# Turning tiles 2 to 15 of x on VectorE, from loads made in 32x32 blocks, instead of on TensorE

## What is computed

```
h  = cond(x);  x = x + ffn(h)          # layer 0: cond = x @ W.T + 2 * gated LoRA (top 2 of 8 experts);
                                       #          ffn  = LoRA of the top-1 expert of 8, rank 16
h  = cond(x);  x = x + ffn(h)          # layer 1: cond = x @ W.T + b + 2 * LoRA of the sequence's slot;
                                       #          ffn  = x @ W_base.T + b_base + 2 * gated LoRA (top 2 of 8)
```

## Time and profile before

| | |
|---|---|
| time before, median of 3 runs | 510.89 us (510.64 to 512.52) |
| span of the profiled execution | 509.9 us, 8653 instructions |
| TensorE matmul busy | 497.2 us (98%), 3119 instructions |
| VectorE busy | 269.8 us (53%), 839 instructions |
| ScalarE busy | 135.9 us (27%), 300 instructions |
| GpSimd busy | 9.5 us (2%), 18 instructions |
| mean traffic of the DMA queues | 79 GB/s; 30397 packets |

### The profile page before, as it was taken

The page is one execution under the profiler, slowest core; times in us unless marked ns, Lnnn a source line. Parts: engine busy times, 40 slices in busy tenths (PEclk is TensorE's granted clock), DMA queues, the critical chain, the costliest instruction groups (busy, mean ns, idle before and its releaser), DMA issues.

```text
span 509.9 us, 8653 instructions
## 1 busy us (share of the span) xinstructions
PE 497.2 (98%) x3119; PEld 475.4 (93%) x3119; DVE 269.8 (53%) x839; ACT 135.9 (27%) x300; POOL 9.5 (2%) x18
## 2 busy tenths in 40 slices
PE   5999999999999989999999999999999999999997
PEld 4977899999999889999999999999999999999997
DVE  3655865444448355465384475466548438446211
ACT  4454620111111332241141132223124113222111
POOL 2040000000000000000000000000000000000000
PEclk9998999999999999999999999999999999999999
DMA  7984722311111131113104104012210410201111
GB/s 236 343 266 154 210 91 84 125 41 42 41 41 47 43 102 46 42 43 105 42 5 144 42 3 145 0 43 65 79 41 2 146 42 3 62 1 45 57 42 41
DMA packets 30397, 40.22 MB, mean 79 GB/s; under 512 B 10487, under 2 KB 22529, under 8 KB 30238
## 3 DMA queue, kind: packets, MB, share of 16 engines
q1 hardware_dynamic: 30094, 39.25, 23.6%
q0 software_dynamic: 272, 0.56, 0.4%
HBM read 28.64 MB, written 11.16 MB: 78 GB/s over the span
## 4 chain that ended last, share of the span: by engine, by line
PE 95%; DMA 2%; DVE 1%; ACT 1%; issue 0%; SPq 0%; POOL 0%; DVEq 0%; ACTq 0%
PE banks L1002 28%; PE banks L1004 27%; PE banks L1003 27%; PE banks L1016 3%; PE banks L997 3%; PE banks L1167 2%; PE banks L1200 1%; DMA wraw<-in_L_cond_W_dram 1%; PE banks L1051 1%; DMA routers<-in_L_ffn_W_router_dram 1%; PE banks L1025 1%; PE banks L1151 0%; PE banks L1205 0%; DVE ws_lo L676 0%; PE banks L1210 0%
## 5 line engine op out<-in xcount | busy, mean ns | idle before, releaser
L1002 PE MATMUL banks<-Mhi,x1Thi 128*128 128x392 f32 x384 | 138.0, 359 | 2.0 <-DVE x1Tlo L676 1.5
L1003 PE MATMUL banks<-Mlo,x1Thi 128*128 128x392 f32 x384 | 130.6, 340 | 0.0
L1004 PE MATMUL banks<-Mhi,x1Tlo 128*128 128x392 f32 x384 | 130.5, 340 | 0.0
L1002 PEld LDWEIGHTS banks<-Mhi,x1Thi 128*128 128x128 f32 x384 | 72.3, 188 | 4.5 <-issue 2.5
L1002 PE MATMUL banks<-WbThi,ws_hi 128*128 128x392 f32 (+2 forms) x216 | 74.7, 346 | 0.0
L1004 PE MATMUL banks<-WbThi,ws_lo 128*128 128x392 f32 (+2 forms) x216 | 73.2, 339 | 0.0
L1003 PE MATMUL banks<-WbTlo,ws_hi 128*128 128x392 f32 (+2 forms) x216 | 73.0, 338 | 0.0
L1003 PEld LDWEIGHTS banks<-Mlo,x1Thi 128*128 128x128 f32 x384 | 72.5, 189 | 0.0
L1004 PEld LDWEIGHTS banks<-Mhi,x1Tlo 128*128 128x128 f32 x384 | 72.2, 188 | 0.0
L1004 PEld LDWEIGHTS banks<-WbThi,ws_lo 128*128 128x128 f32 x216 | 40.7, 188 | 3.2
L1003 PEld LDWEIGHTS banks<-WbTlo,ws_hi 128*128 128x128 f32 x216 | 40.7, 188 | 3.1
(11 more groups left out here) (186 smaller groups left out, 796.7 us busy)
## 6 DMA issues: line engine op xcount, KB each, us to landing
wraw<-in_L_cond_W_dram SPq DMA_DIRECT2D x16, 512.0 KB, 4.4
out_dram<-ybuf SPq DMA_DIRECT2D x15, 512.0 KB, 3.1
xin<-in_x_dram SPq DMA_DIRECT2D x13, 512.0 KB, 4.3
wraw<-in_L_ffn_W_base_dram SPq DMA_DIRECT2D x8, 512.0 KB, 6.5
xin_first<-in_x_dram SPq DMA_DIRECT2D x1, 1024.0 KB, 9.2
x1T_dram<-xin_first SPq DMA_DIRECT2D x1, 1024.0 KB, 3.9
wraw<-x1T_dram SPq DMA_DIRECT2D x2, 512.0 KB, 3.5
Fbuf<-fe_hi_dram SPq DMA_DIRECT2D x16, 64.0 KB
```

Of the source, the lines that this page charges most:

```text
L1002: pe.matmul(out_, l[0], r[0], start=start, stop=False, **kw)
L1003: pe.matmul(out_, l[0], r[1], start=False, stop=False, **kw)
L1004: return pe.matmul(out_, l[1], r[0], start=False, stop=stop, **kw)
```

## The change

- `load_x` and the load of `x2_early` become `load_blocks`: four DMAs for a tile, one for each column group j of 32 numbers. Partition j*32+r, and in it k, i, c, get row i*32+r, column k*128+j*32+c of the tile. Each piece read is 32 numbers (128 bytes), 4096 pieces for a tile.
- VectorE then turns a whole tile with one instruction (`turn_x`): a transpose in 32x32 blocks of 128x1024 numbers, written into one half of `x1_sums`. For tiles n and n+1 it stands behind `split(3)` with a wait for `x1T_lo` (all four quarters of the last pair are split); for tile 2 it stands ahead of the splits of x1 of tiles 0 and 1, behind `m_done` 24; for tile 3 where the low part was formed.
- ScalarE copies the high part from `x1_sums` (SBUF) and not from PSUM, two instructions for a tile as before. For tile n this now stands behind `wzT_part(m + 1)` and still ahead of `y_part(m + 1, 0)`.
- GpSimd forms the low part: 28 subtractions of 128x512. VectorE's 28 instructions for it are gone.
- `x1_add` is one instruction for a quarter, in place, since `x1_sums` already holds the tile of x (tiles 0 and 1 keep the old form as `x1_first`).
- TensorE's 112 transposes of tiles 2 to 15 are gone. In slot 0, `small0(a)` moves from behind step 3 to behind step 10, just ahead of the turning of `hg`.
- SP waits for `x_turned` instead of `tx_done` before a new load of x. `x2_early` gets memory of its own. The scratch area of software DMAs is set to 8192 bytes.

```diff
+            def load_blocks(tile, t, s):
+                src = block_rows(t)
+                for j in range(NJ):
+                    sp.dma_start(tile[j * BLK:(j + 1) * BLK, :].rearrange("r (k i c) -> r k i c", k=K, c=BLK), src[j])\
+                      .then_inc(s, 16)
...
             def load_x(t, turn):
-                sp.dma_start(xin[turn][:, :], xf[bass.ds(t * P, P), :]).then_inc(x_in[turn], 16)
+                load_blocks(xin[turn], t, x_in[turn])
...
+            with gp.Fori(1, NB) as i:
+                for half in range(2):
+                    for h in range(2):
+                        gp.wait_ge(xT_hi, i * 4 + half * 2 + h + 1)
+                        gp.tensor_tensor(half_tiles(xT_main[1], half, h), half_tiles(x1_sums, half, h),
+                                         half_tiles(xT_main[0], half, h).bitcast(F32), ALU.subtract).then_inc(xT_lo, 1)
...
+            def turn_x(t, half, src, s, n):
+
+                dve.wait_ge(s, n)
+                dve.transpose(half_of(x1_sums, half), src[:, :].rearrange("p (k c) -> p k c", k=K)).then_inc(x_turned, 1)
...
+            def x1_add(q, g, bank):
+
+                dve.wait_ge(x1w_done, q * 4 + g + 1)
+                dve.tensor_tensor(quarter(x1_sums, g), bank, quarter(x1_sums, g), ALU.add).then_inc(x1_sum, 1)
...
+            dve.wait_ge(m_done, 3 * K)
+            turn_x(2, 0, x2_early, x2_in, 64)
             for g in range(4):
-                if g == 2:
-                    xT_part(2, 0, xT_main, XT_EARLY)
                 x1T_part(0, 0, g, quarter(wraw[2 + g // 2], g % 2))
...
                     if first:
-                        xT_part(a + 1, 1, xT_main, XT_BANKS[1])
+                        turn_x(a + 1, 1, xin[1], x_in[1], 64)
...
                 if has_n:
-                    xT_part(n, 0, xT_main, XT_BANKS[0])
-                    xT_part(n + 1, 1, xT_main, XT_BANKS[1])
+                    dve.wait_ge(x1T_lo, q * 4 + 4)
+                    turn_x(n, 0, xin[0], x_in[0], b * 64 + 64)
+                    turn_x(n + 1, 1, xin[1], x_in[1], b * 64 + 128)
...
                 pe.wait_ge(as_lo, b + 1)
+                main_to(7)
                 if first:
-                    main_to(0)
                     small0(a, 0, xT_main)
-                main_to(7)
...
                 adapter(m + 1)
-                main_to(40)
-                if has_n:
-                    turn_x_main(n, 0, b + 1, [(x1_half, q * 4 + 2), (x1_half, q * 4 + 3)])
                 main_to(44 if has_n else 46)
...
                 lora(m + 1, 1)
-                if has_n:
-                    turn_x_main(n + 1, 1, b + 2, [(x1_half, q * 4 + 4), (xT_lo, n * 2 + 1)])
                 main_to(48)
```

More of the change, by code:

```diff
@@ L87, in adaln_ffn @@
         wzThi, wzTlo = sb("wzThi", [P, P], F32R), sb("wzTlo", [P, P], F32R)
+        x2_early = sb("x2_early", [P, D])
         def gate_tiles(n):
@@ L268, in adaln_ffn @@
         c0_sums = [t[:, 0:4 * RC].rearrange("p (k c) -> p k c", k=4) for t in (a0f, b1_j)]
[L270 removed]
         XT_FIRST = [(pm[0], pm[1]), (pm[2], pm[0])]
[L272 removed]
+        BLK = 32
+        NJ = P // BLK
         X1W_BANKS, X1W_FIRST = [big[0], big[1], big[2], big[0]], [big[0], big[1], p0, pt]
@@ L283, in half_tiles, with block_rows, half_of @@
             return t[:, :].rearrange("p (k c) -> p k c", k=K)[:, 4 * h:4 * h + 4, half * P:(half + 1) * P]
+        def block_rows(t):
+            return xf[bass.ds(t * P, P), :].rearrange("(i r) (k j c) -> j r k i c", r=BLK, j=NJ, c=BLK)
+        def half_of(t, half):
+            return t[:, :].rearrange("p (k c) -> p k c", k=K)[:, :, half * P:(half + 1) * P]
         def wait_earlier(eng, s, n):
@@ L425, in slot_dmas @@
                     for half in range(2):
-                        sp.wait_ge(tx_done, b * 4 + 10 + half * 2)
+                        sp.wait_ge(x_turned, b * 2 + 3 + half)
                         load_x(b * 2 + 6 + half, half)
-            sp.wait_ge(tx_done, 8)
+            sp.wait_ge(x_turned, 2)
             load_x(5, 1)
@@ L500, in _, with xT_part @@
                 act.activation(C0hi[:, 4 * g:4 * g + 4, ER + E:C0C], c0_sums[g], ACT.Copy).then_inc(c0_hi, 1)
[L502 to L505, removed]
+            def xT_part(t, half, xT, at):
                 for h in range(2):
@@ L508, in xT_part, with xT_turned @@
                             at[h].rearrange("p (k c) -> p k c", k=4), xT_hi)
-            xT_part(0, 0, xT_first, XT_FIRST[0], False)
+            def xT_turned(t, half, guard):
+                if guard:
+                    act.wait_ge(p0_done, t - 1)
+                for h in range(2):
+                    hi_half(x_turned, t - 1, half_tiles(xT_main[0], half, h), half_tiles(x1_sums, half, h), xT_hi)
+            xT_part(0, 0, xT_first, XT_FIRST[0])
             act.wait_ge(d0w_done, 1)
@@ L616, in _ @@
                 if g == 2:
-                    xT_part(2, 0, xT_main, XT_EARLY, False)
+                    xT_turned(2, 0, False)
                 if g == 0:
@@ L631, in slot @@
                 if first:
-                    xT_part(a + 1, 1, xT_main, XT_BANKS[1], False)
+                    xT_turned(a + 1, 1, False)
                 exp1(m)
@@ L652, in slot @@
                     x1T_part(q, 1 - turn, 3, quarter(x1_sums, 3))
+                wzT_part(m + 1)
                 if has_n:
-                    xT_part(n, 0, xT_main, XT_BANKS[0], True)
-                wzT_part(m + 1)
+                    xT_turned(n, 0, True)
                 y_part(m + 1, 0)
@@ L658, in slot @@
                 if has_n:
-                    xT_part(n + 1, 1, xT_main, XT_BANKS[1], True)
+                    xT_turned(n + 1, 1, True)
                 if has_a:
@@ L816, in wzT_part, with x1_first @@
                 lo(wzTlo[:, :], pt_wz, wzThi[:, :]).then_inc(wzT_lo, 1)
-            def x1_add(q, g, bank, xT, sums):
-                dve.wait_ge(x1w_done, q * 4 + g + 1)
-                wait_earlier(dve, x1T_hi, q * 4 + g - 3)
+            def x1_first(g, bank, xT, sums):
+                dve.wait_ge(x1w_done, g + 1)
                 dve.tensor_tensor(quarter(sums, g), bank, quarter(xT[1], g).bitcast(F32), ALU.add).then_inc(x1_half, 1)
-                dve.wait_ge(x1_half, q * 4 + g + 1)
+                dve.wait_ge(x1_half, g + 1)
                 dve.tensor_tensor(quarter(sums, g), quarter(sums, g), quarter(xT[0], g).bitcast(F32), ALU.add)\
                    .then_inc(x1_sum, 1)
+            def x1_add(q, g, bank):
+                dve.wait_ge(x1w_done, q * 4 + g + 1)
+                dve.tensor_tensor(quarter(x1_sums, g), bank, quarter(x1_sums, g), ALU.add).then_inc(x1_sum, 1)
             def x1T_part(q, turn, g, src):
@@ L879, in _ @@
             for g in range(4):
-                x1_add(0, g, X1W_FIRST[g], xT_first, xin_first)
+                x1_first(g, X1W_FIRST[g], xT_first, xin_first)
             dve.wait_ge(bcol_ready, 1)
@@ L938, in add @@
                 def add(g):
-                    x1_add(q, g, X1W_BANKS[g], xT_main, x1_sums)
+                    x1_add(q, g, X1W_BANKS[g])
                 def split(g):
@@ L1158, in _ @@
             pe.wait_ge(bias_step, 3)
[L1160 to L1168, removed]
             def slot(b, turn, has_a, has_n, first=False):
@@ L1230, in slot @@
                 adapter(m)
-                if first:
-                    turn_x_main(a + 1, 1, 1, None)
                 main_to(14)
```

13 lines of the change are left out of this document (5 added, 8 removed).

## The result

The changed kernel took **536.37 us** (median; 535.19 to 537.12) against 511.56 for the kernel before in the same comparison (510.64 to 512.52): a ratio of 1.048, 95% interval 1.046 to 1.051. It is slower, as forecast, but by 25 us where 11 were forecast, and the time lies above the range. The profiled execution has a span of 533.4 us, 23.5 more than before, and its mean granted clock of TensorE is 0.968, against 0.997 before.

What follows compares the result with a forecast made beforehand. The prediction took TensorE's instruction list to bound the kernel: 509.9 us span, minus 12.2 for transposes, plus 23.3 of waits, plus 0.99 outside the span, gave 522.0 us. The range was 517 to 534 us.

Steps and rivals of the forecast that it cites:

- What bounds the kernel, and the transposes (-12.2 us): TensorE's list is 95% of the chain; removing 14 blocks of transposes at 0.87 us saves 12.2 us.
- The turn: VectorE's 128x1024 transpose of a tile, taken as 1.22 us; bounds 0.90 and 2.44.
- GpSimd's subtraction: Low part of a tile, 512 columns: 1.27 us each from start to start, two in a row on the chain.
- The waits: New TensorE stops: 2.69 us at each of borders 1-2 to 5-6, plus border 0-1 and slot 0; 23.3 us.
- border 0-1: Border of slots 0 and 1: less main work behind wz, 3.17 us against a chain of 6.82; wait 3.65 us.
- the start of slot 0: VectorE turns tile 2 before the first split of x1, so TensorE starts 0.56 us later.
- hg: Slot 0: small0(2) moved directly ahead of the hg turn no longer covers the gate chain; wait 2.65 us.
- tile 3: Slot 0: tile 3 turned behind top1(2), chain 6.8 us against TensorE's 3.87; wait 2.95 us.
- The loads, costed at nothing: Loads of x tiles in 4096 pieces: at most 14 us a tile within some 40 us a slot; priced at zero.
- The clock: Rival: TensorE's clock falls in the eight new waits, 1.72 us each, 13.8 us in all, giving 536; chance 0.10.
- granted clock 1.00 throughout the slots: Sign expected in the changed profile: TensorE's clock does not fall anywhere in the slots.
- The outside of the span: Median of the runs above the profiled span of 509.9 us: 0.99 us, added to the sum at the end.

Runs made afterwards that it cites:

- small0_back: The changed kernel with small0 of tile 2 back behind step 3 of slot 0 instead of step 10: 533.84 us, ratio 1.042 to the kernel before.
- with 12 matmuls: The changed kernel with twelve matmuls of 392 columns, result never read, ahead of the first small0 of slots 1 to 6: 526.43 us, ratio 1.028.
- with 6: The changed kernel with six unread matmuls of 392 columns instead of twelve ahead of each border's small0: 528.89 us, ratio 1.032.
- border_fix: The changed kernel with split(2) and split(3) ahead of wzT_part and the first tile's low part on VectorE: 517.53 us, ratio 1.011.
- best: border_fix with slot 0 mended: tile 2 turned between x1's splits, tile 3 before the gates, small0(2) behind step 6: 511.52 us, ratio 0.9995.
- low_on_vector: The changed kernel with the low part of each pair's first tile (and tile 2) formed by VectorE instead of GpSimd: 527.49 us, ratio 1.030.
- best_2: best with as_part moved ahead of the rest of the border's work, so tile n+1's turn ends VectorE's loop: 503.58 us, ratio 0.983.

## Why the prediction was wrong

- **What bounds the kernel, and the transposes (-12.2 us).** Right. They are gone, and nothing on TensorE took their place.
- **The turn.** Predicted 1.22 us from the pass over 1024 columns, measured 1.224. The estimate of 2.49 worked out from the page "VectorE: DVE Perf Modes" of the Trainium skill (section "The three transpose paths") was meant as the most for a tile; the trace shows half of it, one ordinary pass.
- **GpSimd's subtraction.** Predicted 1.27 us, measured 1.309 in the mean, and 5.02 / 4 = 1.26 at the border of slots 2 and 3.
- **The waits.** At the borders 2.60 us four times and 2.50 once for 2.69; at border 0-1 3.62 for 3.65; the start of slot 0 grew by 0.47 for 0.56; `hg` 2.44 for 2.65; tile 3 2.53 for 2.95. In sum 22.0 us for 23.3.
- **The loads, costed at nothing.** Right: a ratio of 1.000 when made alone, and a DMA of a quarter tile lands in 3.8 us.
- **The clock: the step that failed.** The prediction had this rival with its place (the eight new waits) and a price of 1.72 us a fall, and gave it a chance of 0.10. In the sum itself the clock stood at nothing, and that term is what failed: it was 13.7 us. The only ground against it was that the clock stood at 1.00 around the stop of 1.53 us. That row says nothing of stops of 2.65 to 3.65: I carried it past its end. It also ends at 182.00, while that stop lasts until 182.83, so it couldn't show a fall behind it (over 181.3 to 187.3 the kernel before does have 1.00). The forecast "granted clock 1.00 throughout the slots" was wrong in eight of nine places. The terms as measured: 509.9 - 12.2 + 22.0 = 519.7; nine stretches of 1.52 us are 13.7; together 533.4, which is the span of the profile. That the last digit agrees is luck: other executions of the same list differ by up to 2 us, part of the double stretch lies inside its stop and costs nothing, and on the other side a middle slot grew from 41.9 to 44.5 us, 2.65 where 0.95 was forecast; the clock explains 1.5 of the difference, and 0.2 to 0.3 stay open. That the rival's 536 meets the measured time is luck in part too: eight falls at 1.72 for nine stretches at 1.52.
- **The outside of the span**, taken as 0.99 us, was mis-sized by 0.8. The record has span and time of every later execution, and the time is 1.8 to 1.9 us above the span in each, before and after; the 0.99 came from setting the span of one execution against the median of others. Here the median lies 3.0 above the span because the profiled execution, 535.19 us, was the quickest of the four.

"TensorE: Matmul & The Clock Gate" of the Trainium skill, Part 1 ("the default state is throttled, and activity releases the throttle"), gave the right direction, and the trace now agrees: eight of nine stops came with a fall.

**Open.** Why a stop of 2.0, 2.5 or 3.5 us comes with a fall in one execution and not in another wasn't found. Without a fall were the 2.00 us ahead of slot 0 in `small0_back`, the 2.44 for `hg` in the changed kernel, the 2.52 ahead of tile 3 with 12 matmuls (window 203 to 209: 1.00), the 2.54 at border 0-1 with 6 (237 to 243: 1.00), and the 3.53 for `hg` in `border_fix`, where `best` has a fall behind 3.23 and `low_on_vector` behind 3.54 at the same place; so length alone doesn't decide between 2.0 and 3.5 us. That standing still is the cause is shown for the borders, where filling or shortening the stop took the falls away; the falls in the M phase, one to three stretches from run to run, have no such stop ahead of them and stay unexplained. Why the turn at the loop's end shortens the hole is argued, not shown: in `best_2` the first of the three instruction transfers starts while the turn (307.18 to 308.42) is at work, and in `best` only after the last instruction of the loop has ended (311.60), so the turn may cover the loading. How much of the 8 us from `best` to `best_2` belongs to the hole, and how much to `as_part`, is read from the traces (5 us in one slot, 0.5 in each of the others) and wasn't run apart.

## What to carry to other kernels

Where TensorE works without a pause, a new wait of 2 to 3 us is to be priced at its length and a fall of the clock behind it (here 1.5 us each, 60% on top), and a row of a shorter stop is no evidence against that. Here shortening the wait to 1.2 us gave back nearly twice what was cut, and even matmuls whose result nobody reads gave back 10 us. An operation that TensorE did 0.9 us at a time inside its own list was cheap; moved to other engines it paid only when its whole chain (turn, copy, subtraction) ended about when TensorE needed it. Here that took four further edits, and the time then became 1.7% less than before. When an engine's list is reordered, look again at its loop's end: the place behind which it waits for nothing visible can move onto the path.

## What the runs showed of the hardware

- In the changed kernel the granted clock fell at eight stops of 2.00 to 3.62 us of a TensorE that was otherwise busy, for 3.4 us each (6.8 at the longest, from 1 us before its end). In the other kernels single stops of 2.00 to 2.54 us, and one of 3.53, had no fall. With 1.05 to 1.56 us in the slots it stayed at 1.00 every time.
- A stretch of 3.4 us at the lower level costs 1.52 us in a run of matmuls of 272 columns (4.64 against 3.12 us).
- VectorE transposes 128x1024 float32 numbers in 32x32 blocks in 1.224 us, the time of an ordinary pass (1.225 us in the earlier trace rows).
- Reading a tile in 4096 pieces of 128 bytes (52 DMAs of 128 KB each for 13 tiles) changed nothing that could be measured (0.998 to 1.002).
- Behind the way back of its loop VectorE stood still twice for 2.4 to 2.8 us ("issue"), in three kernels (the low part on VectorE, and the two built on it), once for 1.5 to 1.9 in the kernels with matmuls in the waits and with the splits first, and once for about 1 us where the turn of a tile was the loop's last instruction. Transfers of 8192 bytes on the queue of the instructions start inside the two holes, and are gone there when the loop is written out.
